# Attention in front of two local layers: order of the band, the split of the maxima, rings of banks, grouped row loads and the end of the phase are changed

## The reference, cut to what matters

```python
def attention_part(x):                       # per batch b of 4, head h of 16
    n = layernorm(x)
    Q, K, V = heads(n @ Wq.T + bq), heads(n @ Wk.T + bk), heads(n @ Wv.T + bv)
    s = Q @ K.T / 4 + prior_lambda * gaussian_mask(2048)   # band around the diagonal
    o = softmax(s) @ V
    return x + merge(o) @ Wo.T + bo
x = attention_part(x)
x = x + local_layers(layernorm(x))           # 2 layers; not touched
```

## Time and profile before

| | us |
|---|---|
| median of 3 runs | 6016.73 (6012.47 to 6018.92) |
| the profiled execution | 6014.54 |
| its span | 6012.8 |
| PE busy | 5686.9 (95%) |
| DVE busy | 4911.7 (82%) |
| ACT busy | 3789.6 (63%) |
| POOL busy | 2110.1 (35%) |

### The profile page before, as it was taken

How to read it: one execution, slowest core, us unless ns; L and a number is a source line. 1 busy time by engine, 2 the same in 40 slices (tenths; PEclk the granted TensorE clock), 3 DMA queues, 4 the chain that set the end, 5 groups by cost and what they waited for, 6 DMA issues and landing times. The chain is left out here.

```text
span 6012.8 us, 159946 instructions
## 1 busy us (share of the span) xinstructions
PE 5686.9 (95%) x66524; PEld 3480.2 (58%) x66524; DVE 4911.7 (82%) x10369; ACT 3789.6 (63%) x6386; POOL 2110.1 (35%) x1507
## 2 busy tenths in 40 slices
PE   7999999999999999999999699999899799999899
PEld 2433443333443334444443488888788688888787
DVE  6888898888888888989997588888677689888676
ACT  3666665666666666656667477777433577777333
POOL 2011002111011110020000599999311599999222
PEclk9999999999999999999999899999999899999999
DMA  2011001101011110010000355455200345544211
GB/s 92 24 32 43 28 18 46 36 29 37 21 32 38 37 39 29 18 46 18 18 23 8 89 114 116 112 116 115 55 11 6 94 111 114 118 113 110 65 53 46
DMA packets 264518, 341.83 MB, mean 57 GB/s; under 512 B 47520, under 2 KB 167152, under 8 KB 263792
## 3 DMA queue, kind: packets, MB, share of 16 engines
q1 hardware_dynamic: 263792, 331.60, 21.8%
HBM read 104.16 MB, written 41.94 MB: 24 GB/s over the span
## 5 line engine op out<-in xcount | busy, mean ns | idle before, releaser
L590 ACT ACTIVATE a_pr<-a_w 128x1024 f32<-128x1024 f32 x2048 | 2011.4, 1024 | 937.5 <-PE a_w L459 689.9
L697 DVE TENSOR_REDUCE a_mx<-a_b 128x1 f32<-128x512 f32 x2688 | 1735.6, 684 | 265.0 <-PE a_b L440 264.0
L440 PE MATMUL a_b<-a_kp,a_qp 96*32 96x512 bf16 x16384 | 1476.0, 382 | 103.5 <-DVE a_mx L697 49.6
L459 PE MATMUL a_w<-a_qp,a_kp 99*32 99x512 bf16 x16384 | 1257.3, 380 | 45.8 <-ACT a_pr L590 42.3
L695 DVE CUSTOM_DVE_ANT_0 a_junk<-a_b,a_gw 128x512 bf16<-128x512 f32 x1408 | 964.7, 685 | 188.5 <-PE a_b L440 150.7
L490 PE MATMUL a_po<-a_pr,a_v 128*17 128x512 f32 x8192 | 1070.2, 593 | 0.4 <-ACT a_pr L590 0.4
L440 PEld LDWEIGHTS a_b<-a_kp,a_qp 96*32 96x32 bf16 x16384 | 456.7, 95 | 1020.3 <-issue 406.2
L1467 POOL TENSOR_TENSOR l_p<-l_p,l_rc 128x512 f32<-128x512 f32 (+1 forms) x512 | 725.5, 1445 | 25.2 <-DVE l_rc L1382 25.0
L459 PEld LDWEIGHTS a_w<-a_qp,a_kp 99*32 99x32 bf16 x16384 | 441.8, 97 | 498.6 <-ACT a_pr L590 130.3
L1131 PE MATMUL l_G<-l_wqkv,l_hT 128*128 128x512 f32 x2304 | 620.7, 415 | 40.1 <-DVE l_hT L1324 24.5
L800 POOL TENSOR_TENSOR a_rs<-a_ve,a_nh 128x2 f32<-128x2 f32 (+1 forms) x48 | 39.6, 826 | 1752.6 <-DVE a_ve L623 1752.5
(11 more groups left out here) (192 smaller groups left out, 8658.6 us busy)
## 6 DMA issues: line engine op xcount, KB each, us to landing
l_qs<-l_qT SPq DMA_DIRECT2D x512, 128.0 KB, 2.3
l_kh<-l_kT SPq DMA_DIRECT2D x512, 128.0 KB, 2.4
l_kl<-l_kT SPq DMA_DIRECT2D x256, 128.0 KB, 2.4
a_qp<-q_parts SPq DMA_DIRECT2D x384, 64.0 KB, 2.2
a_kp<-k_parts SPq DMA_DIRECT2D x384, 64.0 KB, 2.2
a_xc<-in_x SPq DMA_DIRECT2D x32, 512.0 KB, 3.5
l_tab<-in_rotary SPq DMA_DIRECT2D x128, 128.0 KB, 2.3
q_parts<-a_stage SPq DMA_DIRECT2D x32, 384.0 KB, 2.5
```

What stands on the lines that cost most here:

```text
L440: m = eng.matmul(bk[32 * r:32 * r + 32, :], qp[s][0:96, o:o + 32], kp[s][0:96, c * 512:c * 512 + 512], start=True, stop=True)
L459: m = eng.matmul(wide[u][32 * r:32 * r + 32, c * 512:c * 512 + 512], kp[s][0:99, o:o + 32], qp[s][0:99, u * 1024 + c * 512:u * 1024 + c * ...
L590: eng.activation(pr[(2 * n + u) % NP][:, :], wide[u][:, :], ACT.Exp, scale=0.25).then_inc(s_exp[u], 1)
L697: t = eng.tensor_reduce(mx[g % 2][:, qb, c:c + 1], banks[i], X, ALU.max)
```

## The change

- `band(n, u)` is issued for one half, right behind that half of pass 2.
- DVE keeps only the reduction to nm. POOL makes the three parts of the maxima (`rows(g)`), and ACT copies the transposed rows.
- LEAD is 20 instead of 19, and `rows_at(n)` places the transpose of the rows: in the same step n (13 mod 16) as before, but two steps after the last pass 1 product of the head, not one.
- In steps below 0 the ring has seven banks: the three, and the four of `wide`.
- The order of DVE's work before the loop is another, and POOL makes its four reciprocal roots earlier.
- `pack` issues six loads in place of twelve: 48, 32 and 16 rows for each of `qp` and `kp`, the latter with the same 16 source rows repeated.
- The last two pieces of x go into `late`, which lies in the V buffer that the last batch does not use; they are loaded at step 776. After the loop the `out_T` are issued one pair ahead, `biased` stands ahead of all of them, and the second normalising is DVE's.

```diff
-LEAD = W + 3
+LEAD = W + 4
...
+def rows_at(n):
+    return (n + LEAD) // W if (n + LEAD) % W == 1 and W < n + LEAD <= NS + 1 else 0
+def out_at(n):
+    return n // W if n % W == 1 and n > 1 else 0
...
     for n in range(-LEAD, NS + 1):
+        ring = 7 if n < 0 else 3
...
                 t.take(("p1", g1, qb, c), ring)
...
-    CONST, PACK = 16 * 6, 16 * 12
+    CONST, PACK = 16 * 6, 16 * 6
...
         for n in range(-LEAD, NS + 1):
             pass1(n, 0)
             pass2(n, halves_of(n)[0])
+            band(n, halves_of(n)[0])
             pass1(n, 1)
             pass2(n, halves_of(n)[1])
+            band(n, halves_of(n)[1])
             pass1(n, 2)
-            band(n)
             pv(n - 1)
...
+        out_T(("out_T", NB - 1, 0))
         for w0 in range(0, W, 2):
-            out_T(("out_T", NB - 1, w0))
+            if w0 + 2 < W:
+                out_T(("out_T", NB - 1, w0 + 2))
             out_project(("out_project", NB - 1, w0))
...
+        def rows_T(what):                      # ACT
...
+            act.wait_ge(s_full[i], k)
...
+            eng.activation(row[:, :], banks[i].bitcast(BF16)[0:48, 0:128], ACT.Copy).then_inc(s_free[i], 1)
...
             if (qb, c) == (W - 1, 3):          # DVE
                 dve.wait_ge(s_free[i], k)
-                dve.wait_ge(s_dve, step.on(eng.tensor_reduce(nm[:, :], mx[g % 2][:, :, :], X, ALU.max, negate=True)))
...
-                dve.wait_ge(s_dve, step.on(eng.tensor_copy(pk[:, 0, :], nm[:, :])))
-                dve.wait_ge(s_dve, step.on(eng.tensor_tensor(r1[:, :], nm[:, :], pk[:, 0, :], ALU.subtract)))
-                dve.wait_ge(s_dve, step.on(eng.tensor_copy(pk[:, 1, :], r1[:, :])))
-                eng.tensor_tensor(pk[:, 2, :], r1[:, :], pk[:, 1, :], ALU.subtract).then_inc(s_pk, 1)
-        def rows_T(what):                      # DVE
...
+                    dve.wait_ge(s_pk, g)
+                eng.tensor_reduce(nm[:, :], mx[g % 2][:, :, :], X, ALU.max, negate=True).then_inc(s_nm, 1)
...
+        def rows(g):                           # POOL
+            pool.wait_ge(s_nm, g + 1)
...
+            for k in range(3):
+                src = r1 if k else nm
+                if k == 2:
+                    eng.tensor_tensor(pk[:, 2, :], r1[:, :], pk[:, 1, :], ALU.subtract).then_inc(s_pk, 1)
+                    continue
+                eng.tensor_copy(pk[:, k, :], src[:, :]).then_inc(s_pkpart, 1)
+                pool.wait_ge(s_pkpart, 3 * g + 2 * k + 1)
+                if k == 0:
+                    eng.tensor_tensor(r1[:, :], nm[:, :], pk[:, 0, :], ALU.subtract).then_inc(s_pkpart, 1)
+                    pool.wait_ge(s_pkpart, 3 * g + 2)
...
-            for n, dst, order in (("q", qp[s], QPART), ("k", kp[s], KPART)):
-                for j, p in enumerate(order):
-                    eng.dma_start(dst[16 * j:16 * j + 16, :], parts[n][b, h // 8, p, r0:r0 + 16, :]).then_inc(s_pack[s], 16)
+            for p, j, n in ((0, 0, 3), (1, 3, 2), (2, 5, 1)):
+                eng.dma_start(qp[s][16 * j:16 * j + 16 * n, :], parts["q"][b, h // 8, 0:n, r0:r0 + 16, :]).then_inc(s_pack[s], 16)
+                eng.dma_start(kp[s][16 * j:16 * j + 16 * n, :], parts["k"][b, h // 8, p:p + 1, r0:r0 + 16, :].to_broadcast([n, 16, L])).then_inc(s_pack[s], 16)
...
+            if n == (NB - 1) * S + 8:
+                sp.wait_ge(s_pv, (NB - 1) * S)
+                for i, (b, _, j) in enumerate(LATE):
+                    eng.dma_start(late[b, "o", j], a["x"][b, j * 512:j * 512 + 512, :].rearrange("(w p) d -> p w d", p=128)).then_inc(s_late[i], 16)
```

More of the change, by code:

```diff
@@ L114, in load_chunks @@
             out += [(b + 1, "v", j) for j in range(4)]
-    return out + [(NB - 1, "o", j) for j in range(4)]
+    return out + [(NB - 1, "o", j) for j in range(2)]
+LATE = [(NB - 1, "o", j) for j in range(2, 4)]
 def chunk_units(b, j):
@@ L240, in attention_tables @@
             if p1:
-                t.take(("p1", g1, qb, c), 3)
+                t.take(("p1", g1, qb, c), ring)
         if after:
@@ L247, in attention_tables @@
         if p1:
-            t.take(("p1", g1, qb, 2), 3)
+            t.take(("p1", g1, qb, 2), ring)
         if n in units:
-            unit(units[n], 3)
+            unit(units[n], ring)
             if units[n][0] in HOLDS:
@@ L253, in attention_tables @@
         if p1:
[L254 to L262, removed]
+            t.take(("p1", g1, qb, 3), ring)
+        if rows_at(n):
+            t.take(("rows", rows_at(n) - 1), ring)
+        if out_at(n):
+            t.take(("out", out_at(n) - 1), ring)
+    t.take(("out", NB * HA - 1), 3)
+    unit(("out_T", NB - 1, 0), 7)
     for w0 in range(0, W, 2):
-        unit(("out_T", NB - 1, w0), 7)
+        if w0 + 2 < W:
+            unit(("out_T", NB - 1, w0 + 2), 7)
         unit(("out_project", NB - 1, w0), 7)
@@ L338, in xc_of @@
     def xc_of(key):
-        return xc[where[key] % 2]
+        return late[key] if key in late else xc[where[key] % 2][:, :, :]
     def chunk(what):
@@ L462, in pass2, with band @@
                 m.then_inc(s_wide[u], 1)
-        def band(n):
+        def band(n, u):
             if not 0 <= n < NS:
                 return
[L467 to L475, removed]
-                    m.then_inc(s_wide[u], 1)
+            m = None
+            for q in range(4):
+                for bk, c0, p0, n_ in windows(n % W * 128 + 32 * q):
+                    if bk // 2 == u:
+                        o = wide[u][:, bk % 2 * 512:bk % 2 * 512 + 512]
+                        m = eng.matmul(o[32 * q:32 * q + 32, c0:c0 + n_], sel[:, :], mt[:, p0:p0 + n_], start=False, stop=True, skip_group_check=True)
+            if m:
+                m.then_inc(s_wide[u], 1)
         def pv(n):
@@ L741, in vector @@
             normal(("turned", 0, 0, half))
-        for j in range(1, 4):
+        for half in range(2):
+            normal(("turned", 0, 1, half))
+        for i in range(2):
+            eng.memset(kp[i][96:99, :], 1.0)
+        for j in range(2, 4):
+            stats(("stats", 0, j))
             for half in range(2):
                 normal(("turned", 0, j, half))
-            split_k(("project", 0, 0, j - 1, "k"))
-            if j < 3:
-                stats(("stats", 0, j + 1))
+            split_k(("project", 0, 0, j - 2, "k"))
+        eng.memset(kp[2][96:99, :], 1.0)
+        eng.memset(po[:, :], 0.0).then_inc(s_ones, 1)
         dve.wait_ge(s_const, CONST)
@@ L784, in vector @@
             pass1(n, 3)
-            if n + LEAD - 1 < NS and (n + LEAD) % W == 0 and n > -LEAD:
-                rows_T(("rows", (n + LEAD) // W - 1))
-            if n > 1 and n % W == 1:
-                finish_T(("out", n // W - 1))
+            if out_at(n):
+                finish_T(("out", out_at(n) - 1))
         finish_T(("out", NB * HA - 1))
@@ L874, in gpsimd @@
                 after = units[n] if units[n][0] in ("project", "out_project") else None
+        for j in range(4):
+            biased(NB - 1, j)
         for w0 in range(0, W, 2):
[L876 to L878 removed]
+            rstd(rs2[:, w0 % 4:w0 % 4 + 2], 2)
     def sync(eng):
```

80 lines of the change are left out of this document (49 added, 31 removed).

## The result

The changed kernel takes 5869.49 us (median of 4 runs, 5867.60 to 5870.23) against 6016.75 for the kernel before (4 runs): a ratio of 0.9756, with a 95% interval of 0.9739 to 0.9773. The forecast was 5860. The profiled execution took 5869.88 (6014.54 before), so the sum has 144.7 us to explain where it said 155.

| stage | before | after | gained | forecast |
|---|---|---|---|---|
| up to the first exponential of step 0 | 126.9 | 124.3 | 2.6 | 9 |
| first to last exponential | 3190.9 | 3067.0 | 123.9 | 129 |
| last exponential to the next phase | 50.3 | 30.4 | 19.9 | 17 |
| later phases and what lies around the span | 2646.4 | 2648.2 | -1.8 | 0 |

What follows compares the result with a forecast made beforehand. PE, busy 3051 of 3193 us, loses 3.1 us per head at three places: mid-head, maxima, head's end. 63 + 55 - 2 + 14 - 5 + 0 + 9 + 4 + 17 = 155 off 6014.5; forecast 5860, range 5832 to 5902.

Steps and rivals of the forecast that it cites:

- Band: Mid-head, steps 7 and 8: band beside its half recovers 1.05 of 1.14 us in 60 heads, 63 us (48 to 68).
- last 20 steps: Steps without pass 1: ACT's idle and the last reversals of halves go, gaining 4 us (0 to 7).
- rival C: Every step: short band matmuls between long ones break PE's pace, 0.05 us each, 50 in all: 5910; chance 0.06.
- Maxima and stalls: Maxima cuts leave DVE: 0.88 us at 63 heads, 55; three stalls beside POOL's bias go, 14; POOL's order costs 2.
- rival B: At the maxima the ring, not DVE, sets the price; 0.8 stays instead of 0.35, 40 us less gain: 5900; chance 0.11.
- The 2 for POOL's order: Heads 10, 26 and 42: `project_lo` stands ahead of the cuts on POOL, costing 0.7 us each, 2 in all.
- Rival D: Between reduction and transposes: POOL's cuts are dear, chain 11.9 us against 4.4 spare, PE stands 473: 6333; chance 0.03.
- Six loads: Loads of the parts use few DMA engines: first landing 6.5 us later, heads 8, 24 and 40 lose 5 in all.
- Rival A: Loads spread over all 16 DMA engines, so 8 us at the start and 5 at three heads return: 5847; chance 0.17.
- The start: Before the loop: DVE's new order brings the first load 6.4 us earlier (3 to 9), cancelled by 6.5 later landing: 0.
- Seven banks: Pass 1 alone, below step 0: the stretch falls from 65.4 to 56 us, gaining 9 (0 to 13).
- End: Eight pairs after the loop: no wait for the bias behind a load, 2.75 us per pair, gaining 17 (12 to 18).

Runs made afterwards that it cites:

- x_first: Changed kernel with x's fourth piece loaded ahead of the first stores of the parts, and the next two behind heads 0 and 1's part loads: 5863.18 us.
- The two orders of the last section: Changed kernel with SP's x loads reordered before the loop, 5863.18 us; then also DVE's splits of K's third and fourth piece ahead of last memsets and scaling, 5863.24.

## Why the prediction was right, and where it was not

It said 5860 and the median is 5869.5, inside the range. The mechanisms of the loop stand; the difference has one main place, the start. That the total came so near is in part luck: 9 lost at the first load and 5 in the loop stand against 3 won at the banks and 3 at the end.

*Band* (forecast 63) and *last 20 steps* (forecast 4): 63.0 by the median, 61.7 in the loop without the lower clock of head 48, and this has the last head in it. A head without units gives back 1.14, where 1.05 was forecast; of the heads with units some give back far less (0.3 in heads 9 and 25). The last head took 32.1 instead of 33.4, and all of that goes back with the band. That no pace would be lost (rival C excluded) held: 2.66 per ordinary step.

*Maxima and stalls* (55 - 2 + 14 = 67): what is left of the loop's 123.9, with 61.7 for the band and 5.7 lost at the rows, is 67.9, if the parts add up. Undone, less comes back: 49.3 by the median with the cuts back, 52.8 in its profile, and the copy costs a head without units nothing. Per such head 0.91 was gained against the kernel before, as forecast (0.88), so rival B falls. Of it only 0.6 returns with the cuts alone; what the added step brings was not tried by itself. The stalls: heads 10, 26 and 42 gained 17.6 together, 11.5 more than three heads without units, where the forecast had 14 - 2 = 12. With the cuts back they lose 9.4, only 7.5 more than three such heads. The difference goes with the clock: before, it fell in all three heads, with the cuts back in one, and where it stays up such a stall costs 2.1. The 2 for POOL's order were not paid, for PE does not wait there. POOL's cut took 0.20 to 0.22, less than the 0.35 taken from bigger ones. Rival D's spare time of 4.4 is measured as 4.2, but its price was too simple: with POOL 3.75 later, 35.5 of the 57.4 us that the loop lost are in seven heads, where PE waits 1.95 to 3.35 us and the clock falls behind it.

*Six loads* (6.5 at the start, 5 in three heads): 7.2 and 5.7; undone, 12.2 by the median against 11.5. Rival A is excluded by the completions and by the 14.5. The Trainium skill ("DMA: Bandwidth & Descriptors", Rules for kernel authors) states the rule; the trace agrees with 9600 packets.

*The start* (the failed step). The forecast had the first load 6.4 earlier, with 3 as the worst case; it was 2.4 later. It read DVE's queue, where `split_k` stood ahead of the statistics, and took it that moving it would move the fourth piece of x as well. But that piece is issued by SP, behind a store of K's parts: at 25.93, where it was 26.57. DVE then waited 4.52 for it. What DVE still won (4.3 at those statistics) went in the queue behind: splits beside POOL's reads take 1.64 and 1.53 instead of 0.69, and two memsets and the scaling stand ahead of the third split. So the last store went out at 50.61, 0.3 later than before, and landed 4.9 later instead of 2.7, with a 512 KB load issued 1.6 ahead of it; before, that load was 5.7 ahead, and with the load moved behind (`x_first`) it is 2.9. The two orders of the last section take these apart: SP's gives 7.1 back at the first load, DVE's 3.0 more, the latter by the profile alone.

*Seven banks* (9): 12.2 for the stretch, with one step more in it, and 15 for the ring itself.

*End* (17): 19.9, for the most part as a pair takes 2.51 on DVE and not 2.75.

Sum of what was measured, against the sum forecast: 5 less in the loop (the band and the last steps), 6 less up to step 0 (9 less at the first load and 1 at the six loads, 3 more at the banks), 3 more at the end, and 2 of scatter in phases that were not edited: 10.

## What to carry to other kernels

Before a step is moved earlier on one engine, follow its input to the queue that issues it, and what stands ahead of it there. A load's time goes by how many engines its outermost source dimension can use: fewer issues are no gain where somebody waits for the landing, and cheap where nobody does. Where two engines alternate over a small ring, take short work off the one that has no idle, and measure how long the other may take: here it was free up to 4.2 us, and 0.6 beyond cost 0.5. Before two heads, or two kernels, are compared by a few microseconds, look at the clock of both: here 6.8 us at the lower level made one of three equal stalls cost 5.1 instead of 2.1.
